# Loads moved ahead across four stage boundaries of a decoder kernel, with one tile in two of the residual add moved to another engine

## The reference, cut to what matters

```python
x = _layernorm(x + _L0_attn_ref(x, ...))              # 4-bit quantised attention
x = _layernorm(x + _L0_xattn_ref(x, ctx, mask))       # cross attention over ctx
x = _layernorm(x + _L0_ffn_ref(x, Wg, Wu, Wd, ...))   # gated feedforward, low-rank experts
x = _layernorm(x + _L1_attn_ref(x, Wq, ..., Wo, bo))  # attention, 8 dimensions by 64 heads
x = _layernorm(x + _L1_xattn_ref(ctx, ctx, x, ...))   # long convolution
x = _layernorm(x + _L1_ffn_ref(x, w1, ..., b2))       # ternary feedforward
```

## Time and profile before

| | us |
|---|---|
| median of 3 runs | 2073.99 |
| lowest, highest | 2070.40, 2074.09 |
| the profiled execution, its own time | 2073.55 |
| span of that execution in the trace | 2071.8 |

### The profile page before, as it was taken

How to read it: one execution, slowest core, us unless ns; L and a number is a source line. 1 busy time by engine, 2 the same in 40 slices (tenths; PEclk the granted TensorE clock), 3 DMA queues, 4 the chain that set the end, 5 groups by cost and what they waited for, 6 DMA issues and landing times. The chain is left out here.

```text
span 2071.8 us, 33036 instructions
## 1 busy us (share of the span) xinstructions
PE 1787.9 (86%) x12302; PEld 1369.8 (66%) x12302; DVE 1419.0 (68%) x2841; ACT 994.4 (48%) x1678; POOL 514.4 (25%) x535
## 2 busy tenths in 40 slices
PE   4489999685759999999999996999998699768886
PEld 2256665324549999999999975777876577524443
DVE  8478888565935566566566554566666588639997
ACT  3436666523415444444444433432443244459995
POOL 5233331182110000000000001000100399723321
PEclk9679999857979999999999997999998899869998
DMA  5499885205522222221222214221322544020011
GB/s 162 50 100 98 95 94 63 103 0 177 191 79 64 60 75 61 69 80 56 75 77 60 65 49 174 101 82 62 103 72 72 117 106 99 31 112 11 16 26 31
DMA packets 149890, 166.54 MB, mean 80 GB/s; under 512 B 46368, under 2 KB 100512, under 8 KB 147936
## 3 DMA queue, kind: packets, MB, share of 16 engines
q1 hardware_dynamic: 143076, 151.85, 32.2%
q10 hardware_dynamic: 6656, 12.58, 1.6%
HBM read 117.91 MB, written 21.05 MB: 67 GB/s over the span
## 5 line engine op out<-in xcount | busy, mean ns | idle before, releaser
L1571 ACT ACTIVATE f_gate<-f_gu 128x256 f32<-128x256 f32 x264 | 98.3, 381 | 270.4 <-PE f_gu L1446 189.2
L1696 DVE TENSOR_TENSOR f_hid<-f_gate,f_gu 128x256 f32<-128x256 f32 x264 | 108.4, 421 | 155.4 <-ACT f_gate L1571 152.3
L567 DVE TENSOR_REDUCE a_rowmax<-a_ring 128x2 f32<-128x512 f32 x256 | 165.0, 687 | 51.8 <-PE a_ring L649 49.4
L2578 PE MATMUL e_py<-e_kv,e_toep 128*128 128x288 f32 x640 | 163.4, 412 | 15.5 <-DVE e_kv L2605 15.2
L520 ACT ACTIVATE a_prob<-a_sT 128x1024 f32<-128x1024 f32 x128 | 130.5, 1026 | 48.4 <-PE a_sT L638 48.4
L2578 PEld LDWEIGHTS e_py<-e_kv,e_toep 128*128 128x128 f32 x640 | 121.3, 193 | 47.5 <-issue 16.1
L1459 PE MATMUL f_gu<-f_lowh,f_bg 128*128 128x256 f32 x704 | 141.3, 283 | 5.2 <-POOL f_lowl L1371 5.0
L1446 PE MATMUL f_gu<-f_xhi,f_wg 128*128 128x256 f32 x704 | 131.1, 284 | 0.0
L1446 PE MATMUL f_gu<-f_xhi,f_wu 128*128 128x256 f32 x704 | 130.2, 283 | 0.0
L1701 DVE TENSOR_TENSOR f_hl<-f_hid,f_hh 128x768 fp32r<-128x768 f32 (+2 forms) x90 | 84.7, 941 | 55.9 <-ACT f_hh L1614 54.8
L1459 PEld LDWEIGHTS f_gu<-f_lowh,f_bg 128*128 128x128 f32 x704 | 115.8, 191 | 9.7 <-POOL f_lowl L1371 5.2
(11 more groups left out here) (419 smaller groups left out, 4866.0 us busy)
## 6 DMA issues: line engine op xcount, KB each, us to landing
f_entry<-in_WdT SPq DMA_DIRECT2D x89, 256.0 KB
d_staging<-in_w SPq DMA_DIRECT2D x16, 1024.0 KB, 5.8
a_qs<-a_hi SPq DMA_DIRECT2D x64, 128.0 KB, 7.2
a_ks<-a_hi SPq DMA_DIRECT2D x64, 128.0 KB, 6.1
e_toep<-lags SPq DMA_DIRECT2D x16, 512.0 KB, 3.8
f_entry<-in_Bg SPq DMA_DIRECT2D x89, 64.0 KB
f_entry<-in_Bu SPq DMA_DIRECT2D x89, 64.0 KB
cf<-in_xT SPq DMA_DIRECT2D x4, 1024.0 KB, 8.1
```

The source lines that it names most:

```text
L567: dve.tensor_reduce(rowmax[:, s % 2, :, e * SLOTS + j], ring[n % RING][:, :].rearrange("p (q t) -> p q t", t=T), AX.X, ALU.max, negate=Tru ...
L1571: act.activation(gate[:, i % 2, :], gu[n % 3][:, 0, :], ACT.Silu).then_inc(s_["gate_ready"], 1)
L1696: dve.tensor_tensor(hid[:, j, :], gate[:, i % 2, :], gu[n % 3][:, 1, :], ALU.mult).then_inc(s_["hid_ready"], 1)
L2578: last = pe.matmul(py[n % RING][:, 0:YS], toep[:, u, h % 2, (t - j) * P:(t - j + 1) * P], kv[:, h % 2, j, :, :].rearrange("p b c -> p (b c ...
```

## The change

1. `attention0_finish` issues, behind its own loads of x, the mask, the context of three batches and five weight pieces that `cross_attention` used to load first (12 transfers), and waits for them. The space comes from tensors of the first attention that are now released one stage part earlier. `cross_attention` issues none of them.
2. In the same loop the add of each odd tile moves from GpSimd's list to VectorE's, between the take-out and the quantising.
3. The normalised x of the first three batches stays on chip through the feedforward; `cross_attention` doesn't store it and `expert_feedforward` doesn't load it. The first two entries of expert weights (six transfers) are loaded at the end of `cross_attention`, and `weights_high(0)` stands behind the two reads of the transposed x.
4. Late in the feedforward x3 of batch 0 and the matrices W1q and W1k are loaded. Its tail transposes x3 into PSUM banks that are free by then, makes high and low parts of both, at addresses that `attention1` takes over, and loads W1v and W1o into the same staging buffers. `attention1` starts with the split of W1v (index 2) and with the projections; W1o is split after the last high part of batch 0's keys. Its loads are the biases and x only.

```diff
 RING, RR = 4, 8
 SPAN = KT * NC
-held = ExitStack()
-xt = Maker(nc, held).sb("x_rows1", [P, NT, D], side="right")
-keep["rows1"].update(held=held, rows=xt)
+first, held = ExitStack(), ExitStack()
+fix = Maker(nc, held)
+rows = (Maker(nc, first).sb("x_first", [P, EARLY * TB, D], side="right"),
+        fix.sb("x_rows1", [P, NT - EARLY * TB, D], side="right"))
+ct = fix.sb("c_ct", [P, CT, TB, D], side="right")
+cf = fix.sb("c_cf", [P, CT, KT, T], side="right")
+mask8 = fix.sb("c_mask8", [P, B, T], mybir.dt.uint8, side="right")
+raw = fix.sb("c_raw", [P, RAW, 6 * P], side="right")
+keep["rows1"].update(first=first, held=held, rows=rows, ct=ct, cf=cf, mask8=mask8, raw=raw)
...
+    sp.dma_start(batch_of(rows, b), io["x"][b * T:(b + 1) * T, :].rearrange("(n p) f -> p n f", p=P)
                  ).then_inc(got_x[b], 16)
+sp.dma_start(mask8[:, :, :], io["mask"].unsqueeze(0).broadcast_to([P, B, T])).then_inc(s_["ahead"], 16)
+for b in range(CT):
+    load_context(sp, io, ct, cf, b, s_["ahead"])
+for n in range(RAW):
+    load_weights(sp, io, raw, n, s_["ahead"])
+sp.wait_ge(s_["ahead"], 16 * (1 + 2 * CT + RAW))
...
 for i in range(B + 1):
-    for q in range(TB):
-        n = i * TB + q
-        if n < NT:
-            if q == 0:
-                pool.wait_ge(got_x[i], 16)
-            pool.wait_ge(s_["y_ready"], n + 1)
-            pool.tensor_tensor(xt[:, n, :], r[:, n % RR, :], xt[:, n, :], ALU.add
-                               ).then_inc(s_["sum_ready"], 1)
+    if i < B:
+        n = i * TB
+        pool.wait_ge(got_x[i], 16)
+        pool.wait_ge(s_["y_ready"], n + 1)
+        pool.tensor_tensor(row_of(rows, n), r[:, n % RR, :], row_of(rows, n), ALU.add
+                           ).then_inc(s_["sum_even"], 1)
...
+if i < B:
+    n = i * TB + 1
+    dve.wait_ge(got_x[i], 16)
+    dve.wait_ge(s_["y_ready"], n + 1)
+    dve.tensor_tensor(row_of(rows, n), r[:, n % RR, :], row_of(rows, n), ALU.add
+                      ).then_inc(s_["sum_odd"], 1)
...
-           vv=mk.sb("a1_vv", [P, 2, TB, HEADS0 // 2, 32]))
-attention0_prepare(nc, io, sem, own)
-attention0_core(nc, io, sem, own)
+           factor=mk.sb("a1_factor", [P, 3, KT, NC]))
+with ExitStack() as early:
+    mk = Maker(nc, early)
+    own.update(ks=[mk.sb(f"a1_ks{n}", [P, HEADS0 // 2, T], F32R) for n in range(2)],
+               vv=mk.sb("a1_vv", [P, 2, TB, HEADS0 // 2, 32]))
+    attention0_prepare(nc, io, sem, own)
...
-load_x(0)
-sp.dma_start(mask8[:, :, :], io["mask"].unsqueeze(0).broadcast_to([P, B, T])).then_inc(s_["got_mask"], 16)
-load_x(1)
-load_x(2)
-for n in range(RAW):
-    load_piece(n)
+    sp.wait_ge(s_["w_low"], n - RAW + 1)
...
+for e in range(2):
+    load_entry(sp, io, own["entry"], e, s_["got_entry"])
 sp.wait_ge(s_["got_small"], 32)
+sp.wait_ge(s_["got_entry"], 96)
...
+entry, xt = own["entry"], own["xt"][:, :, :].rearrange("p (u q) f -> p u q f", q=TB)
...
-xlo = mk.sb("f_xlo", [P, 2, KT, T], F32R)
+gap_at = keep["front"] + 12 * KT * D * 4
+xhi = [mk.at(gap_at, "f_xhi0", [P, KT, T], F32R), mk.sb("f_xhi1", [P, KT, T], F32R)]
+xlo = [mk.at(gap_at + KT * T * 4, "f_xlo0", [P, KT, T], F32R), mk.sb("f_xlo1", [P, KT, T], F32R)]
...
+for e in range(2, NS + 1):
+    sp.wait_ge(s_["entry_split"], e - 1)
+    load_entry(sp, io, entry, e, got_entry[e % 2])
+    if e == (B - 1) * FT + 3:
+        sp.wait_ge(s_["a_done"], B)
+        sp.wait_ge(gu_done[0], (B - 1) * FT)
+        for n in range(2):
+            load_attention(n, nstaging[n], s_["got_nw"])
+for n in range(2, 4):
+    sp.wait_ge(s_["nw_low"], 2 * n - 2)
+    load_attention(n, nstaging[n - 2], s_["got_more"])
+sp.wait_ge(s_["got_more"], 32)
...
+for n in range(2):
+    for h in range(2):
+        pool.wait_ge(s_["nw_high"], 2 * n + h + 1)
+        part = slice(h * KT // 2, (h + 1) * KT // 2)
+        pool.tensor_tensor(nw[1][:, n, part, :], nstaging[n][:, part, :], nw[0][:, n, part, :],
+                           ALU.subtract).then_inc(s_["nw_low"], 1)
...
+def turn_next(q):
+    if q == 0:
+        pe.wait_ge(s_["got_next"], 16)
+    pe.wait_ge(s_["hid_ready"], INDEX[NS - 1 + q, 2] + 1)
+    dst = gu[(NS - 3 + q) % 3][:, :, :].rearrange("p w t -> p (w t)")
+    for k in range(KT):
+        last = pe.transpose(dst[:, k * P:(k + 1) * P], xt[:, 2, q, k * P:(k + 1) * P], keep["ident"][:, :])
+    last.then_inc(s_["nx_turned"], 1)
...
+if t == NS + 1:
+    turn_next(0)
+    turn_next(1)
...
-for b in range(XT):
-    load_x(b)
-weights_high(0)
+def next_high(n, h):
+    act.wait_ge(gu_done[0], NS)
+    act.wait_ge(s_["got_nw"], 32)
+    part = slice(h * KT // 2, (h + 1) * KT // 2)
+    act.activation(nw[0][:, n, part, :], nstaging[n][:, part, :], ACT.Copy).then_inc(s_["nw_high"], 1)
 x_raw(0, 0)
 x_raw(0, 1)
+weights_high(0)
 powers(0)
...
+    if t == (B - 1) * FT:
+        act.wait_ge(stored[2], 32)
+        act.dma_start(xt[:, 2, :, :], rows("x3", 0)).then_inc(s_["got_next"], 16)
+    if t in (NS, NS + 1):
+        next_high(0, t - NS)
+for q in range(TB):
+    act.wait_ge(s_["nx_turned"], q + 1)
+    src = gu[(NS - 3 + q) % 3][:, :, :].rearrange("p w t -> p (w t)").rearrange("p (k t) -> p k t", k=KT)
+    act.activation(nxh[:, :, q * P:(q + 1) * P], src, ACT.Copy).then_inc(s_["nx_high"], 1)
+next_high(1, 0)
+next_high(1, 1)
 store_x(B - 1)
...
 take_two(B - 1)
 for q in range(TB):
+    dve.wait_ge(s_["nx_high"], q + 1)
+    src = gu[(NS - 3 + q) % 3][:, :, :].rearrange("p w t -> p (w t)").rearrange("p (k t) -> p k t", k=KT)
+    dve.tensor_tensor(nxl[:, :, q * P:(q + 1) * P], src, nxh[:, :, q * P:(q + 1) * P], ALU.subtract
...
 ring_at[item, owner(step, item)] = len(ring_at)
...
+sp.dma_start(beta[:, :, :], io["b1qk"]).then_inc(s_["beta_in"], 16)
+load_x(1)
+sp.dma_start(vrow[:, :], io["b1v"].broadcast_to([P, D])).then_inc(s_["rows_in"], 16)
+sp.dma_start(orow[:, :], io["bo1"].broadcast_to([P, D])).then_inc(s_["rows_in"], 16)
 load_x(0)
-for n, name in enumerate("qkvo"):
-    if n >= 2:
-        sp.wait_ge(s_["w_split"], n - 1)
-    sp.dma_start(staging[:, n % 2, :, :], io[f"W1{name}"].rearrange("(k p) o -> p k o", p=P)
-                 ).then_inc(piece_in[n % 2], 16)
-    if n == 1:
-        sp.dma_start(beta[:, :, :], io["b1qk"]).then_inc(s_["rows_in"], 16)
-        sp.dma_start(vrow[:, :], io["b1v"].broadcast_to([P, D])).then_inc(s_["rows_in"], 16)
-        sp.dma_start(orow[:, :], io["bo1"].broadcast_to([P, D])).then_inc(s_["rows_in"], 16)
-for b in range(1, XT):
+for b in range(2, XT):
     load_x(b)
...
-pool.wait_ge(s_["ring_read"], ring_at["x1", b] + 1)
+if b:
+    pool.wait_ge(s_["ring_read"], ring_at["x1", b] + 1)
+else:
...
-if half == 0:
-    pe.wait_ge(s_["w_split"], wi + 1)
-    if wi == 0:
-        pe.wait_ge(s_["ring_read"], ring_at["x1", b] + 1)
+if half == 0 and wi == 0 and b:
+    pe.wait_ge(s_["ring_read"], ring_at["x1", b] + 1)
...
-act.wait_ge(piece_in[n % 2], 16 * (n // 2 + 1))
-act.activation(w[0][:, n, :, :], staging[:, n % 2, :, :], ACT.Copy).then_inc(s_["w_high"], 1)
+act.activation(w[0][:, n, :, :], staging[n % 2][:, :, :], ACT.Copy).then_inc(s_["w_high"], 1)
```

251 lines of the change are left out of this document (130 added, 121 removed).

## The result

The changed kernel took 2039.1 us, the median of four executions (2036.50, 2038.18, 2040.01 and, profiled, 2051.19), and the one before 2073.2 beside it. The ratio is 0.984, its 95% interval 0.981 to 0.987: 34 us faster, where 25.5 were forecast and 2042 was the low end of the range. The profiled execution alone gained 22.4, 2051.19 against 2073.55. So the forecast stood between two readings of one result, and the executions' spread is the first thing to explain. With all later runs there are 16 executions of the changed kernel: 12 between 2036 and 2043, one at 2046, three between 2048 and 2051; and 61 of the one before: 11 between 2060 and 2065, 50 between 2070 and 2079. Each kernel has a shorter and a longer length, 10 to 12 us apart. (One later execution, of late_entry, at 2156.7 and a mean granted clock of 0.80, was disturbed and is left out.)

The account below looks back on a forecast made before the run. TensorE, busy 86%, was taken to lose time at stage boundaries and in attention0_finish, where it waits for GpSimd. 2073.55 - 5.7 - 3.5 - 6.2 - 10.8 + 0.7 = 2048.05, say 2048.0 us; range 2042 to 2057.

Parts of the forecast that it names:

- C: Feedforward's start: waits for x (4.2 us) and for the first expert weights (2.0) both go, a gain of 6.2 us.
- D: Start of attention1: the first projection needs only the set-up, a gain of 10.8 us, bounds 9.5 and 11.5.
- E: Feedforward's tail: W1o's load shares the queues with the last store, a cost of 0.7 us, between 0 and 3.
- A: attention0_finish: one add of two moves from GpSimd to VectorE, net gain 5.7 us, bounds 4.4 and 9.9.
- B: cross_attention: scores start without waiting for the context's load, a gain of 3.5 us, bounds 0 and 4.2.
- the clock's rival: Feedforward's start: the clock stays low; 35 us of full-clock work so slowed would give 2083 us; chance 0.04.

Follow-up runs that it names:

- late_entry: Changed kernel with the first two expert-weight entries loaded behind the barrier again and weights_high(0) ahead of the reads of transposed x: 2048.87, 2053.70, 2055.58 us, and 2156.7 disturbed.
- again2: The changed kernel, unaltered, run again with a second profile: 2036.53 (profiled), 2038.35, 2039.67, 2039.80, 2045.83, 2042.63 us.
- late_ctx: Changed kernel with mask, context and five weight pieces loaded by cross_attention itself again, behind the barrier: 2045.84, 2047.34, 2053.81, 2054.58 us.
- again: The changed kernel, unaltered, run for more executions: 2048.45 (profiled), 2036.35, 2037.64, 2037.64, 2036.66, 2049.68 us.
- pool_add: Changed kernel with the add of each odd tile back on GpSimd: 2041.67, 2042.13, 2042.92, 2043.40, 2043.70, 2053.09 us.
- old_again: The kernel before the change, unaltered, run for a second profile of it: 2070.5 us.
- shift5: Changed kernel with one set-up copy of the second attention made six times, starting it 2.5 us later: 2049.26, 2050.68, 2051.14, 2053.22, 2054.43, 2054.78 us.
- late_wo: Changed kernel with W1o loaded by the second attention's own list instead of in the feedforward's tail: 2043.76, 2043.86, 2045.05, 2048.40 us.

## Why the prediction was right and wrong

- **The steps that held.** C measured 6.6 for 6.2, D 10.8 for 10.8, E +0.5 to +0.7 for +0.7 in the two profiles of the table, and +0.1 to +1.0 over all with W1o's load in the tail. D was read from the traces alone; no run undid it.
- **A, a step that failed.** I wrote "Net gain 5.7 us", with 4.4 as the lower bound. The stretch from the loop's first bias subtraction to the next stage shortened by 3.9. The step charged each moved add to GpSimd's chain, as if GpSimd alone set the pace. But in the full steps its distance didn't fall to 8.1, it stayed 8.78, because GpSimd now waits 1.99 us a step for VectorE. What shortened was the loop's beginning: up to the last bias subtraction 61.4 us became 57.0, and the end took 0.5 more. VectorE's quantising and add stand still for 1.7 and 1.1 us beside GpSimd's subtraction and add; in the row of before the payment was on GpSimd's side. The Trainium skill, page "SBUF — State Buffer", section "Who interferes with whom", has the two exclude each other for whole instructions. In kind the trace agrees, 2.92 us against 1.22 in the earlier trace rows; in sum, the measured 3.9 lies below the 4.4 by that page and further below my 5.7.
- **B, a step that failed.** I wrote "3.5 us", and above it "4.2 if the clock rises with more in hand". The scores moved by 3.7, but in again2 the first tile is added 5.1 earlier (5.5 by late_ctx), since the clock also rises sooner (1.4 us, the rest of 5.1). There the term was mis-sized by 1.6, and its upper bound too low; in the first profile, with 4.1, it was within its bounds. That the sum of the five steps, 25.8 in again2 and 24.6 in the first profile, came so near 25.5 is luck: A was 1.8 too high and B up to 1.6 too low.
- **The step that put the total out of the range.** "Nothing but those four places is touched by the change; the 88 feedforward steps and the middle of the attention keep their lists." True of the lists, not of the time. The forecast put every other stage at nothing. In again2 the stages behind the first projection are 9.4 us shorter, which turns 27.7 into 37.1. The end of `cross_attention` varies too: from the first tile added to the last it takes 75.1 us in again, again2, pool_add and old_again, and 76.5 to 76.8 in before, the first profile and late_ctx. So both kernels have both values. A forecast made as a difference of sums assumed the same clock in both kernels wherever the work is the same, and it was made against 2073.55, which is an execution of the longer length.
- **Why 34 and not 25.5.** Length against length the change is worth 24: the long executions average 2049.8 against 2073.4, the short ones (with the one at 2042.6) 2038.3 against 2062.2. The other 10 of the medians' 34 come from the mixture: 50 of 61 executions of the kernel before are long, 12 of 16 of the changed kernel short. The kernel before, run beside every group of experiments, has medians from 2072.4 to 2073.2 in all of them, so the group isn't the reason. That the shares can depend on where a stage starts is shown by shift5; why the changed kernel's place is mostly the good one, and what decides in one execution, is open. No rival of mine held this; the clock's rival was on the slow side only, and at the feedforward's start, where the clock rose 11 us behind the set-up (0.60 in the window from 582 to 587 of the first profile).

## What to carry to other kernels

Take several profiles before a change is costed, and compare distances between marks, stage by stage: only so does the share of untouched stages show. Let the stretch of an edit begin at a mark right ahead of it: from the start of the span pool_add read 5.3 us, from the loop's first bias subtraction 3.9, the same within 0.1 in all profiles. Where TensorE's clock falls at short waits, an edit that gains 0.5 us in its stretch may come with executions 5 slower (late_wo, four of them), and a delay of 2.5 with 13 (shift5), so judge an edit by its own stretch and by the distribution of many executions, not by one median. Work taken across a barrier gave what the waits ahead of it had shown (3.7, 6.6 and 10.8 us), and 1.4 more at one place with the earlier clock. An operation moved off an engine gave 3.9 where its price on that engine's chain said 5.7, since the other engine then set the pace.
